# Splitting queries and keys before the transposition, with the orders of all engines rewritten

## The chip, the cores and the metric

The kernel runs on one core of a Trainium2 chip. The metric is the device time of one launch in microseconds (us). Five engines work side by side, each through its own list of instructions in order: TensorE (PE), VectorE (DVE), ScalarE (ACT), GpSimd (POOL) and SyncE (SP, which here only issues DMA). They wait for each other by semaphores.

## The reference, cut to what matters

```python
h = concat([tok(x), txt], axis=1)       # 64 images; 196 patches + 32 text rows = 228 tokens of 192
xn = norm_scale * layernorm(h) + norm_bias
q, k, v = split(xn @ W_attn + b_attn)   # 12 heads of 16
q, k = rope(q), rope(k)                 # o0 = x0*cos - x1*sin ; o1 = x0*sin + x1*cos
att = softmax(concat([sink, causal(q @ k.T / 4)]))[..., 1:]
h = h + (att @ v @ W_proj + b_proj) * rezero
xf = layernorm(h)                       # mixture of 8 experts, the best 2 of each token
out = h + sum over 2 experts of w * expert(xf)     # a token keeps its slot while an expert has room
```

`tok` sums each 16x16 patch of 12 channels and multiplies by a 12x192 matrix. Everything is float32. The products of queries and keys, which feed an exponential, are formed from two parts of each number: the number rounded to the short format `fp32r`, and the remainder. So a head has 64 rows on the contraction side: 16 numbers in the four pairings of high and low parts.

## The kernel before, in words

The kernel has two passes. Pass 1 goes through the 64 images ("batches"), from the patches to the attention, the gate and the scatter of each token's row into the expert's list in HBM. Pass 2 goes through the lists of the 8 experts. The change touches pass 1 alone.

Pass 1 is a pipeline written by hand. One **step** of it works on five batches at once, each one stage further: `p` (image folded on POOL, pooled on DVE), `a` (layernorm, the product that gives q and k, the rotation), `m` (q and k turned so that a head's numbers lie along partitions, then first scores and their maxima), `t` (scores once more, transposed, exponentials, attention, projection) and `z` (second layernorm, gate, choice of two experts, slots, scatter). `batches()` gives them; `steps()` runs 6 steps unrolled, then a loop of two steps at a time to 64, then 4 steps of emptying. In a step, the order of instructions on each engine is that of `step_tensor`, `step_scalar`, `step_vector` and `pass1_gpsimd`, written out by hand. T0 to T5 are the six turns of q and k (`turn_qk`; even numbers turn q, odd ones k), S0 to S8 the nine transposed scores (`score_t`), and `score` 0 to 8 the first scores. These 24 products use the PSUM banks 0 to 3 in a ring (`RING`, `bank_free`): each may start when the product four places before it has been read. Banks 4 and 5 hold the attention, 6 and 7 the rest.

What the change touches, by name:

- `make_qk(t)` (L847) multiplies the normalized tokens of half `t` by the weights of q and k; half 0 goes to bank 6, half 1 to bank 7. `rotate` (L533, L535) multiplies the result by cosine and sine into `rot_c` and `rot_s` on DVE. `add_rotation` (L723) adds the two on POOL, in two instructions a half, and writes each sum four times into `qk`: 768 elements a partition each.
- `turn_qk` (L892) transposes four blocks of `qk` in float32. `round_qk` (L775, ACT) copies the turned bank to `rounded` as `fp32r`. `split_qk` (L550, L556, DVE) reads `rounded` and the bank and writes high or low part into `q_t` (two instructions of 64 partitions) or `k_t` (one of 128).
- `norm1_stats`, `norm2_stats` (DVE), `inverse_std` (POOL, four small dependent instructions for each of the two norms) and `norm1_apply`, `norm2_apply` (ACT, L738, L746) make the two layernorms. `turn_xn` (L838), `copy_xn` (L759) bring the first one to `make_qk`.
- `gate_logits` (L1015, PE), `choose` (L620 to L635), `weigh` (L641 to L656) and `assign` (L663 to L679, all DVE) are the gate; `hot_sum` (L635) and `seen` (L677, L679) add two operands that both lie in SBUF. `scatter_waits` (L1272) issues four indirect DMAs from POOL's queue, behind `routed` and `row_whole`.
- `fold_image` (L686, POOL, three of 896 elements), `pool_image` (L502, DVE), `spread_patches` (L694, POOL), `sum_channels` (L829, PE), `copy_h` (L731, L732, ACT) are the patches.

## Time and profile before

| | us |
|---|---|
| median of 3 runs | 3273.91 |
| lowest, highest | 3270.16, 3279.08 |
| the profiled execution, whole | 3278.84 |
| its span (first to last instruction) | 3277.0 |
| pass 1, to the last scatter's landing | about 2036 |

The page of the profile gives the busy time of each engine, the chain that ended last and the costliest groups of instructions. For a pipeline like this one the useful views are those of a single step: the timeline of each engine, with the idle time ahead of an instruction and what ended it. An engine's busy time includes time in which an instruction had started and stood, so a long duration may itself be a wait.

### The profile page before, as it was taken

The page shows a single profiled execution, that of the slowest core. Times are in us where ns is not written, and L with a number is a line of the kernel's source. Part 1 is how long each engine was busy: PE and PEld are TensorE (multiplying, and loading weights), DVE is VectorE, ACT ScalarE, POOL GpSimd, SP SyncE. Part 2 cuts the span into 40 slices and gives each one's busy share as a digit, 9 for nine tenths or more (in the row PEclk, how much of TensorE's full clock was granted, in tenths as well). Part 3 has the DMA queues.
Part 4 walks back from the last instruction along what each step waited for, and adds up shares of the span by engine and source line. Part 5 has one row for each costly group of instructions (what it writes and reads, how often), then busy time and mean ns, then how long its engine had stood idle before and what let it go on. Part 6 is the DMA issues. An engine that isn't in the chain of part 4 may idle for free.

```text
span 3277.0 us, 62705 instructions
## 1 busy us (share of the span) xinstructions
PE 2888.8 (88%) x20432; PEld 2525.7 (77%) x20432; DVE 2329.4 (71%) x5748; ACT 1389.0 (42%) x3462; POOL 2082.0 (64%) x1814
## 2 busy tenths in 40 slices
PE   2888888888888888888888885999999999999997
PEld 1777777777777777777777774898988889898987
DVE  3888898898889889888988983445444545454453
ACT  0444444444444444444444443434343434443443
POOL 2677777777777777777777762455555555555555
PEclk9999999999999999999999996999999999999999
DMA  6545544433343343343333301333343343333333
GB/s 191 150 140 147 160 142 142 134 102 87 105 107 89 97 106 103 86 105 107 89 97 106 105 26 48 58 50 66 47 68 65 50 67 46 68 48 68 49 65 47
DMA packets 205961, 297.49 MB, mean 91 GB/s; under 512 B 88374, under 2 KB 167675, under 8 KB 205874
## 3 DMA queue, kind: packets, MB, share of 16 engines
q1 hardware_dynamic: 82994, 243.82, 26.9%
q0 software_dynamic: 122880, 52.55, 11.5%
q8 instruction: 50, 0.82, 0.1%
q14 instruction: 37, 0.30, 0.0%
HBM read 201.73 MB, written 93.90 MB: 90 GB/s over the span
## 4 chain that ended last, share of the span: by engine, by line
issue 29%; POOL 27%; PE 18%; DMA 13%; DVE 7%; ACT 4%; POOLq 1%; SPq 1%; DVEq 0%; ACTq 0%
DMA out<-arena,who 11%; POOL out L1441 8%; POOL qk L723 7%; POOL moe_rows L1272 6%; POOL spread L694 3%; DVE arena L1423 2%; PE bank L847 2%; PE bank L892 2%; PE bank L965 2%; ACT xn L738 2%; POOL rstd L707 1%; PE bank L1413 1%; PE bank L1015 1%; PE bank L838 1%; ACT prob L793 1%
## 5 line engine op out<-in xcount | busy, mean ns | idle before, releaser
L1441 POOL DMA_INDIRECT out<-arena,who x320 | 598.1, 1869 | 203.5 <-issue 199.3
L723 POOL TENSOR_TENSOR qk<-rot_c,rot_s 114x768 f32<-114x768 f32 x256 | 456.4, 1808 | 240.7 <-DVE rot_s L535 238.2
L1399 ACT ACTIVATE arena<-bank 128x456 f32<-128x456 f32 x320 | 175.5, 549 | 629.8 <-PE bank L1390 625.0
L1413 PE MATMUL bank<-prob,arena 128*114 128x192 f32 x2560 | 429.3, 326 | 0.0
L686 POOL TENSOR_TENSOR arena<-arena 112x896 f32<-112x896 f32 x192 | 396.5, 2092 | 44.6 <-DMA arena<-in_x 44.6
L1413 PEld LDWEIGHTS bank<-prob,arena 128*114 128x114 f32 x2560 | 412.2, 178 | 0.0
L1405 DVE TENSOR_TENSOR arena<-bank,arena 128x456 f32<-128x456 f32 x320 | 201.6, 630 | 263.9 <-ACT arena L1399 261.6
L1272 POOL DMA_INDIRECT moe_rows<-row,slot x256 | 293.0, 1144 | 103.1 <-issue 103.1
L571 DVE TENSOR_REDUCE top<-bank 114x2 f32<-114x456 f32 (+1 forms) x576 | 331.7, 623 | 1.8 <-PE bank L907 1.7
L1430 POOL TENSOR_TENSOR rms<-rms,minus_half 114x4 f32<-114x4 f32 x82 | 85.3, 1040 | 351.1 <-DVE rms L1328 351.1
L1386 PE MATMUL bank<-pieces 128*128 128x456 f32 x640 | 256.7, 401 | 44.4 <-DVE arena L1405 39.0
L550 DVE SCALAR_TENSOR_TENSOR pieces<-rounded,split,bank 64x456 fp32r<-64x456 f32 x384 | 261.6, 681 | 15.2 <-ACT rounded L775 10.1
L502 DVE TENSOR_REDUCE pooled<-arena 112x14 f32<-112x896 f32 x192 | 207.2, 1079 | 81.7 <-POOL arena L686 81.7
L1335 DVE COPY w_slot<-arena 114x4 f32 (+1 forms) x81 | 13.8, 171 | 331.8 <-DMA out<-arena,who 331.7
L790 ACT ACTIVATE prob<-bank 115x456 f32<-115x456 f32 x384 | 211.0, 550 | 88.4 <-PE bank L941 88.4
L775 ACT ACTIVATE rounded<-bank 128x456 fp32r<-128x456 f32 x384 | 210.6, 549 | 69.6 <-PE bank L892 68.7
L1388 PE MATMUL bank<-pieces 128*128 128x456 f32 x640 | 239.8, 375 | 0.0
L1390 PE MATMUL bank<-pieces 128*128 128x456 f32 x640 | 239.6, 374 | 0.0
L1387 PE MATMUL bank<-pieces 128*128 128x456 f32 x640 | 239.5, 374 | 0.0
L1389 PE MATMUL bank<-pieces 128*128 128x456 f32 x640 | 238.9, 373 | 0.0
L892 PE MATMUL bank<-ident,qk 114*128 114x114 f32 x1536 | 224.0, 269 | 5.8 <-POOL qk L723 5.8
L847 PE MATMUL bank<-w_qkv,xn_t 97*114 97x384 f32 x512 | 197.4, 509 | 21.7 <-DVE slot L674 21.1
(167 smaller groups left out, 7119.6 us busy)
## 6 DMA issues: line engine op xcount, KB each, us to landing
arena<-in_x SPq DMA_DIRECT2D x64, 2352.0 KB, 11.3
arena<-moe_rows SPq DMA_DIRECT2D x82, 363.4 KB
moe_rows<-filler SPq DMA_DIRECT2D x20, 1453.5 KB
out<-h SPq DMA_DIRECT2D x64, 171.0 KB
out<-arena,who POOLq DMA_INDIRECT x320, 5.1
arena<-in_w_t SPq DMA_DIRECT2D x9, 512.0 KB, 6.7
arena<-in_w_t SPq DMA_DIRECT2D x18, 256.0 KB, 7.2
moe_rows<-row,slot POOLq DMA_INDIRECT x256, 3.3
```

Of the source, the lines that this page charges most:

```text
L550: ins = nc.vector.scalar_tensor_tensor(out=dst, in0=hi[lo, :].bitcast(fp32).rearrange("p (a n) -> p a n", a=2), scalar=split[lo, 0:1], in1 ...
L571: nc.vector.tensor_reduce(dst, src, AX.X, ALU.max).then_inc(maxed[k], 1)
L686: nc.gpsimd.tensor_tensor(xin[at.par][:, g, 0:mid], xin[at.par][:, g, 0:mid], xin[at.par][:, g, mid:XF], ALU.add).then_inc(x_folded, 1)
L723: nc.gpsimd.tensor_tensor(dst, a, b, ALU.add).then_inc(qk_rotated[t], 1)
L847: ins = nc.tensor.matmul(bank[6 + t][0:TT, 0:2 * D], xn_t[:, c, TT * t:TT * (t + 1)], w_qkv[:, c, 0:2 * D], start=(c == 0), stop=(c == 1))
L892: ins = nc.tensor.transpose(dst[:, TT * (2 * a + t):TT * (2 * a + t + 1)], src, ident[0:TT, 0:TT])
L1272: nc.gpsimd.indirect_dma_start(out=moe_rows[0:SLOTS, :], out_offset=bass.IndirectOffsetOnAxis(ap=slot[at.par][:, 2 * t + k:2 * t + k + 1], ...
L1386: nc.tensor.matmul(dst, hi[:, 0, col], za_hi[:, :], start=True, stop=False)
L1388: nc.tensor.matmul(dst, lo[:, 0, col], za_hi[:, :], start=False, stop=False)
L1390: ins = nc.tensor.matmul(dst, lo[:, 1, col], zb[:, :], start=False, stop=True)
L1413: ins = nc.tensor.matmul(bank[6 + s // 2][0:TT, D * (s % 2):D * (s % 2 + 1)], hid[:, j, TT * s:TT * (s + 1)], w_dn[e_par][:, j, :], start= ...
L1441: nc.gpsimd.indirect_dma_start(out=out[:, :], out_offset=bass.IndirectOffsetOnAxis(ap=who[par][:, s:s + 1], axis=0), in_=ys[par][:, s, :], ...
```

## The change

- After `add_rotation`, which now adds in place and once (`rot_c`), ACT rounds the sum into the high places of `qk` (`high_parts`), and POOL subtracts to get the low ones (`low_parts`). `qk` is `fp32r`, and the turn is an `fp32r` product with a unit matrix. What comes out needs only a copy: `place_q` on ACT (two instructions) for q, `place_k` on DVE (one) for k. `round_qk` and `split_qk` are gone.
- Both halves of `make_qk` use bank 6, so the second waits for `rotate(0)`, and `make_v` for `rotate(1)`. Bank 7 is left to the shift and the gate.
- The orders in a step are new on PE, ACT, DVE and POOL. The scatter of a batch is issued one step later, at the head of POOL's step, and pass 1 on POOL has one step more.

The orders in a step, where it matters here. PE: T0, `turn_shift`, `sum_channels`, T1, S0, T2, S1, S2, T3, S3, S4, `attend` 0, T4, `turn_xn`, S5, `make_qk` 0, `turn_xf`, S6, `attend` 1, `make_qk` 1, `gate_logits`, T5, S7, S8, `score` 0, `rank`, `score` 1, `attend` 2, and the rest. ACT: q of T0, shift, `copy_h`, S0, q of T2, S1, S2, S3, `norm1_apply`, S4, `copy_xn`, `norm2_apply`, q of T4, S5, `copy_xf`, S6, `exp_gap`, `high_parts` 0, S7, S8, `keep_h`, `copy_y`, `high_parts` 1, `copy_yn`, `copy_v`. DVE: shift, both statistics and `place_k` 1 and 3, `rotate` 0, `choose`, `rotate` 1, `place_k` 5, maximum 0, `pool_image` 0, maximum 1, `weigh`, `pool_image` 1, maximum 2, `normalize`, `assign`, maxima 3 to 5, `pool_image` 2, maxima 6 to 8, `make_shift`, `residual`. The diff shows the start of each of these lists.

```diff
+        qk = sb("qk", [TT, 2, 2 * HEADS, 4, HD], fp32r)
         val = [sb(f"val{i}", [TT + 1, 2, HEADS, 32]) for i in range(2)]
-        rounded = [sb(f"rounded{i}", [128, 4 * TT], fp32r) for i in range(2)]
...
-            wait(dve, qk_rotated[t], 2 * at.b)
-            src = bank[6 + t][0:TT, 0:2 * D]
+            wait(dve, qk_low[t], at.b)
+            src = bank[6][0:TT, 0:2 * D]
...
-        def split_qk(dve, at, r):
-
-            dve.wait_ge(qk_rounded, 6 * at.b + r + 1)
...
+        def place_q(act, at, r):
+
+            act.wait_ge(qk_turned[r], at.b + 1)
+            if r == 0:
+                wait(act, scored_t[8], at.b - 1)
             k = TURNS[r]
-            if r == 0:
+            src = bank[bank_of("turn", r)]
+            for side in range(2):
+                lo = slice(64 * side, 64 * side + 64)
+                dst = q_t[at.par][lo, :, :].rearrange("p (a s) n -> p a s n", s=2)[:, 2 * k:2 * k + 2, side, :]
+                ins = nc.scalar.activation(dst, src[lo, 0:4 * TT].rearrange("p (a n) -> p a n", a=2), ACT.Copy)
+            ins.then_inc(qk_placed[r], 1)
...
+        def place_k(dve, at, r):
+
+            dve.wait_ge(qk_turned[r], at.b + 1)
+            if r == 1:
                 wait(dve, scored_t[8], at.b - 1)
...
-            else:
-                kk = k - 3
-                dst = k_t[at.par][:, 2 * kk:2 * kk + 2, :, 0:TT].rearrange("p a t n -> p (a t) n")
-                ins = nc.vector.scalar_tensor_tensor(
-                    out=dst, in0=hi[:, :].bitcast(fp32).rearrange("p (a n) -> p a n", a=4), scalar=split[:, 1:2],
-                    in1=src[:, 0:4 * TT].rearrange("p (a n) -> p a n", a=4), op0=ALU.mult, op1=ALU.add)
-            ins.then_inc(qk_split[r], 1)
+            kk = TURNS[r] - 3
+            dst = k_t[at.par][:, 2 * kk:2 * kk + 2, :, 0:TT].rearrange("p a t n -> p (a t) n")
+            src = bank[bank_of("turn", r)][:, 0:4 * TT].rearrange("p (a n) -> p a n", a=4)
+            nc.vector.tensor_copy(dst, src).then_inc(qk_placed[r], 1)
...
         def add_rotation(pool, at, t):
-            n = at.b + 1
-            pool.wait_ge(qk_read[t], n)
-            if t == 0:
-                wait(pool, qk_turned[5], at.b)
+
+            pool.wait_ge(qk_read[t], at.b + 1)
             for half in range(2):
-                dst = qk[:, t, :, :, 8 * half:8 * half + 8]
-                a = rot_c[:, t, :].rearrange("p (a s k) -> p a s k", s=2, k=8)[:, :, half, :].unsqueeze(2)
-                b = rot_s[:, t, :].rearrange("p (a s k) -> p a s k", s=2, k=8)[:, :, 1 - half, :].unsqueeze(2)
-                a, b = (v.to_broadcast([TT, 2 * HEADS, 4, 8]) for v in (a, b))
-                nc.gpsimd.tensor_tensor(dst, a, b, ALU.add).then_inc(qk_rotated[t], 1)
-
+                c, sn = (r[:, t, :].rearrange("p (a s k) -> p a s k", s=2, k=8)[:, :, i, :]
+                         for r, i in ((rot_c, half), (rot_s, 1 - half)))
+                ins = nc.gpsimd.tensor_tensor(c, c, sn, ALU.add)
+            ins.then_inc(qk_rotated[t], 1)
+
+        def low_parts(pool, at, t):
+
+            pool.wait_ge(qk_high[t], at.b + 1)
+            for hi, lo, of, first in piece_views(t):
+                ins = nc.gpsimd.tensor_tensor(lo, of, first.bitcast(fp32), ALU.subtract)
+            ins.then_inc(qk_low[t], 1)
+
+        def piece_views(t):
+
+            for side in range(2):
+                heads = slice(HEADS * side, HEADS * (side + 1))
+                of = rot_c[:, t, D * side:D * (side + 1)].rearrange("p (a k) -> p a k", k=HD)
+                of, first = (v.unsqueeze(2).to_broadcast([TT, HEADS, 2, HD]) for v in (of, qk[:, t, heads, 0, :]))
+                if side == 0:
+                    parts = qk[:, t, heads, :, :].rearrange("p a (c s) k -> p a s c k", s=2)
+                else:
+                    parts = qk[:, t, heads, :, :].rearrange("p a (s c) k -> p a s c k", s=2)
+                yield parts[:, :, 0, :, :], parts[:, :, 1, :, :], of, first
+
+
+        def high_parts(act, at, t):
+
+            act.wait_ge(qk_rotated[t], at.b + 1)
+            wait(act, qk_turned[5], at.b)
+            for hi, lo, of, first in piece_views(t):
+                ins = nc.scalar.activation(hi, of, ACT.Copy)
+            ins.then_inc(qk_high[t], 1)
...
-                wait(pe, routed, at.b - 2)
+                pe.wait_ge(qk_read[0], n)
             for c in range(2):
-                ins = nc.tensor.matmul(bank[6 + t][0:TT, 0:2 * D], xn_t[:, c, TT * t:TT * (t + 1)], w_qkv[:, c, 0:2 * D],
...
-            pe.wait_ge(qk_read[0], n)
+            pe.wait_ge(qk_read[1], n)
...
-                pe.wait_ge(qk_rotated[1], 2 * n)
-                pe.wait_ge(qk_rotated[0], 2 * n)
+                pe.wait_ge(qk_low[1], n)
+                pe.wait_ge(qk_low[0], n)
...
-                    ins = nc.tensor.transpose(dst[:, TT * (2 * a + t):TT * (2 * a + t + 1)], src, ident[0:TT, 0:TT])
+                    ins = nc.tensor.matmul(dst[:, TT * (2 * a + t):TT * (2 * a + t + 1)], src, ident_r[0:TT, 0:TT],
+                                           start=True, stop=True)
...
-            pe.wait_ge(qk_read[1], after(at))
+            wait(pe, routed, at.b - 1)
...
-            half1("S0 T2 S1 S2 T3")
+            half1("T1 S0 T2 S1 S2 T3 S3 S4")
+            if t:
+                attend(pe, t, 0)
+            half1("T4")
+            if a:
+                turn_xn(pe, a)
+            half1("S5")
+            if a:
+                make_qk(pe, a, 0)
...
-            half1("S0 T2 S1")
+            half1("S0 T2 S1 S2 S3")
+            if a:
+                norm1_apply(act, a)
+            half1("S4")
+            if a:
+                copy_xn(act, a)
...
         def step_vector(dve, p, a, m, t, z):
-            if m:
-                split_qk(dve, m, 0)
             if t:
                 split_shift(dve, t)
             if z:
                 norm2_stats(dve, z)
             if m:
-                split_qk(dve, m, 1)
+                place_k(dve, m, 1)
             if a:
...
                 rotate(dve, a, 0)
             if z:
-                assign(dve, z)
+                choose(dve, z)
+            if a:
+                rotate(dve, a, 1)
             if m:
-                split_qk(dve, m, 5)
...
         def pass1_gpsimd(pool):
             def one(half, par, known=None, fill=None):
                 p, a, _, t, z = batches(half, par, known)
+                done = Batch(half, par, 5) if known is None or 0 <= known - 5 < B else None
+                if done:
+                    scatter_waits(pool, done, fill)
+                if a:
+                    inverse_std(pool, a, norm1)
                 if z:
                     inverse_std(pool, z, norm2)
-                if a:
-                    inverse_std(pool, a, norm1)
                 if p:
-                    for g in range(NG):
-                        fold_image(pool, p, g)
+                    fold_image(pool, p, 0)
+                    fold_image(pool, p, 1)
                 if a:
                     add_rotation(pool, a, 0)
-                if z:
-                    scatter_waits(pool, z, fill)
+                if p:
+                    fold_image(pool, p, 2)
                 if a:
+                    low_parts(pool, a, 0)
                     add_rotation(pool, a, 1)
+                    low_parts(pool, a, 1)
                 if p:
                     spread_patches(pool, p)
...
-            for i in range(B, B + 4):
+            for i in range(B, B + 5):
...
```

How instructions lie in a row, at three places. POOL, one step inside the loop of pass 1, from the folds to the spreading (the scatter is `moe_rows`). Before:

```order
L686 TENSOR_TENSOR arena<-arena 112x896 [waits x_loaded0] x3
L723 TENSOR_TENSOR qk<-rot_c,rot_s 114x96x8 [waits qk_turned5,qk_read0]
L723 TENSOR_TENSOR qk<-rot_c,rot_s 114x96x8
L1262 ISA
L1268 REGISTER_ALU [waits filled0]
L1272 DMA moe_rows<-row,slot 36480x204 [waits row_whole,routed]
L1272 DMA moe_rows<-row,slot 36480x204 x3
L723 TENSOR_TENSOR qk<-rot_c,rot_s 114x96x8 [waits qk_read1]
L723 TENSOR_TENSOR qk<-rot_c,rot_s 114x96x8
L693 ISA
L694 TENSOR_TENSOR spread<-pooled,patch 112x196 [waits x_pooled]
```

After, the same stretch; the third fold stands between the addition and the subtraction of half 0:

```order
L686 TENSOR_TENSOR arena<-arena 112x896 [waits x_loaded0] x2
L719 TENSOR_TENSOR rot_c<-rot_c,rot_s 114x24x8 [waits qk_read0]
L719 TENSOR_TENSOR rot_c<-rot_c,rot_s 114x24x8
L686 TENSOR_TENSOR arena<-arena 112x896 [waits x_loaded0]
L726 TENSOR_TENSOR qk<-rot_c,qk 114x24x16 [waits qk_high0]
L726 TENSOR_TENSOR qk<-rot_c,qk 114x12x32
L719 TENSOR_TENSOR rot_c<-rot_c,rot_s 114x24x8 [waits qk_read1]
L719 TENSOR_TENSOR rot_c<-rot_c,rot_s 114x24x8
L726 TENSOR_TENSOR qk<-rot_c,qk 114x24x16 [waits qk_high1]
L726 TENSOR_TENSOR qk<-rot_c,qk 114x12x32
L693 ISA [waits h_summed]
L694 TENSOR_TENSOR spread<-pooled,patch 112x196 [waits x_pooled]
```

The scatter has left this stretch, and each half waits for ACT (`qk_high`). It stands now at the head of the step, POOL after:

```order
L1268 UNCONDITIONAL_BRANCH
L1282 ISA [waits filled1]
L1286 DMA moe_rows<-row,slot 36480x204 [waits row_whole,routed]
L1286 DMA moe_rows<-row,slot 36480x204 x3
L703 ISA
L705 TENSOR_TENSOR var<-mv,ln_eps 114x2 [waits ln1_done,ln1_step]
```

So the first layernorm's `inverse_std` stands right behind the scatter. DVE, the middle of a step in the loop, where the gate and the rotation meet (`best` is the gate's choice, `pieces` is where q and k are split). Before:

```order
L635 TENSOR_TENSOR hot_sum<-hot 114x16
L540 REGISTER_ALU
L550 SCALAR_TENSOR_TENSOR pieces<-rounded,split,bank 64x2x228 x2
L641 TENSOR_SCALAR gden<-gexp 114x2
L642 REGISTER_ALU
L643 RECIPROCAL gw<-gden 114x2
L644 REGISTER_ALU
L645 TENSOR_TENSOR gw<-gexp,gw 114x2
L648 TENSOR_TENSOR wpick<-hot,gw 114x32
L651 REGISTER_ALU
L652 TENSOR_TENSOR row<-wpick 114x2x8
L653 CAST row<-token 114x2
```

`rotate` of half 0 follows there, and right behind it `assign`. After:

```order
L533 TENSOR_TENSOR rot_c<-bank,cos 114x384
L535 TENSOR_TENSOR rot_s<-bank,sin 114x384
L620 MAX best<-bank 114x8 x2
L624 MAX_INDEX best_i<-best,bank 114x8 x2
L627 CAST bank<-best_i 114x4
L628 ISA
L629 TENSOR_TENSOR hot<-small,bank 114x32
L633 REGISTER_ALU
L635 TENSOR_TENSOR hot_sum<-hot 114x16
L533 TENSOR_TENSOR rot_c<-bank,cos 114x384
L535 TENSOR_TENSOR rot_s<-bank,sin 114x384
L559 CAST pieces<-bank 128x4x114
```

Both rotations now lie around the choice, and what was a split in two instructions is one copy from PSUM, for k alone. The gate's weights and the slots come later in the step, behind maxima.

## Rows read from the trace of the kernel before

**Rows 1.** Busy time by stretch, middle of pass 1: each engine's us and (instructions).

```profile
core 0: us, PE busy (x) PEld busy (x) DVE busy (x) ACT busy (x) POOL busy (x), PEclk, DMA share, GB/s
900.00:1100.00 200.00, 175.05 (x1434) 146.79 (x1434) 180.49 (x428) 90.02 (x201) 145.39 (x150) 1.00 0.39 101
```

**Rows 2.** Line L578, one per step: duration ns min/median/max, first and last start.

```profile
L578 DVE TENSOR_TENSOR shift<-top,sink_tok x64: 207/689/1682, 102.1 to 1990.6; 114x48 f32<-114x48 f32 x64
```

**Rows 3.** POOL timeline, one step: start, us, instruction, count, [idle before <-releaser].

```profile
911.64 1.47 POOL L694 TENSOR_TENSOR spread<-pooled,patch 112x196 f32<-112x196 f32 x3
916.13 0.20 POOL L705 TENSOR_TENSOR var<-mv,ln_eps 114x2 f32<-114x2 f32 x1 [3.02 <-DVE mv L519]
...
919.12 6.21 POOL L686 TENSOR_TENSOR arena<-arena 112x896 f32<-112x896 f32 x3
929.10 3.56 POOL L723 TENSOR_TENSOR qk<-rot_c,rot_s 114x768 f32<-114x768 f32 x2 [3.77 <-DVE rot_s L535]
932.87 1.20 POOL L1272 DMA_INDIRECT moe_rows<-row,slot  x1 [0.21 <-issue]
...
938.37 3.57 POOL L723 TENSOR_TENSOR qk<-rot_c,rot_s 114x768 f32<-114x768 f32 x2
```

**Rows 4.** DVE timeline, the same step.

```profile
922.59 0.25 DVE L620 MAX8 best<-bank 114x8 f32<-114x8 f32 x2 [0.26 <-PE bank L1015]
...
923.83 1.54 DVE L635 TENSOR_TENSOR hot_sum<-hot 114x16 bf16<-114x16 f32 x1
925.29 1.38 DVE L550 SCALAR_TENSOR_TENSOR pieces<-rounded,split,bank 64x456 fp32r<-64x456 f32 x2
...
928.00 0.56 DVE L533 TENSOR_TENSOR rot_c<-bank,cos 114x384 f32<-114x384 f32 x1
...
928.94 0.17 DVE L663 TENSOR_SCALAR over<-bank 114x16 f32<-114x16 f32 x1
...
929.88 1.04 DVE L677 TENSOR_TENSOR seen<-seen,hot_sum 114x8 bf16<-114x8 bf16 x1
930.95 1.73 DVE L679 TENSOR_TENSOR seen<-seen,hot_sum 114x8 bf16<-114x8 bf16 x1
932.60 0.68 DVE L556 SCALAR_TENSOR_TENSOR pieces<-rounded,split,bank 128x456 fp32r<-128x456 f32 x1
933.20 1.07 DVE L502 TENSOR_REDUCE pooled<-arena 112x14 f32<-112x896 f32 x1
...
936.20 0.22 DVE L593 RECIPROCAL rden<-bank 114x12 f32<-114x12 f32 x1
...
937.39 2.24 DVE L571 TENSOR_REDUCE top<-bank 114x4 f32<-114x456 f32 x4
```

**Rows 5.** ACT timeline, the same step.

```profile
919.54 0.98 ACT L738 ACTIVATE xn<-h,shifted,rstd 114x192 f32<-114x192 f32 x2
...
921.28 0.55 ACT L759 ACTIVATE xn_t<-bank 97x456 f32<-97x456 f32 x1
```

**Rows 6.** PE timeline, the same step.

```profile
920.57 0.63 PE L838 MATMUL bank<-ident,xn 114*97 114x114 f32 x4 [0.62 <-ACT xn L738]
...
921.56 0.87 PE L1015 MATMUL bank<-gate,xf_t 96*114 96x8 f32 x8
922.37 0.61 PE L965 MATMUL bank<-prob,val 115*32 115x228 f32 x8
...
923.11 0.61 PE L892 MATMUL bank<-ident,qk 114*128 114x114 f32 x4
...
924.33 1.50 PE L847 MATMUL bank<-w_qkv,xn_t 97*114 97x384 f32 x4
925.37 0.67 PE L938 MATMUL bank<-pieces 128*115 128x456 f32 x1
```

**Rows 7.** DVE timeline while pass 1 empties.

```profile
2001.46 0.17 DVE L635 TENSOR_TENSOR hot_sum<-hot 114x16 bf16<-114x16 f32 x1
...
2005.37 0.16 DVE L679 TENSOR_TENSOR seen<-seen,hot_sum 114x8 bf16<-114x8 bf16 x1
```

**Rows 8.** POOL timeline behind it.

```profile
2006.37 1.18 POOL L1272 DMA_INDIRECT moe_rows<-row,slot  x1 [11.64 <-issue]
```

More of the change, by code:

```diff
@@ L766, in copy_v @@
                                  bank[6][0:TT, 0:2 * D].rearrange("p (a k) -> p a k", k=HD), ACT.Copy).then_inc(v_ready, 1)
-        def round_qk(act, at, r):
-            n = at.b + 1
-            act.wait_ge(qk_turned[r], n)
-            if r >= 2:
-                act.wait_ge(qk_split[r - 2], n)
-            else:
-                wait(act, qk_split[r + 4], at.b)
-            nc.scalar.activation(rounded[r % 2][:, :], bank[bank_of("turn", r)][:, 0:4 * TT], ACT.Copy).then_inc(qk_rounded, 1)
         def round_shift(act, at):
@@ L1079, in step_tensor @@
             if m:
-                score(pe, m, t, 3)
-            if m:
-                for k in range(4, 6):
+                for k in range(3, 6):
                     score(pe, m, t, k)
@@ L1086, in step_tensor @@
             if m:
-                score(pe, m, t, 6)
-                score(pe, m, t, 7)
-                score(pe, m, t, 8)
+                for k in range(6, 9):
+                    score(pe, m, t, k)
             if t:
@@ L1145, in step_vector @@
             if m:
[L1146 to L1156 removed]
+                place_k(dve, m, 3)
             if a:
@@ L1159, in step_vector @@
             if z:
-                assign(dve, z)
+                choose(dve, z)
+            if a:
+                rotate(dve, a, 1)
             if m:
-                split_qk(dve, m, 5)
+                place_k(dve, m, 5)
+                max_scores(dve, m, 0)
+            if p:
+                pool_image(dve, p, 0)
+            if m:
+                max_scores(dve, m, 1)
+            if z:
+                weigh(dve, z)
             if p:
@@ L1173, in step_vector @@
                 normalize(dve, t, 1)
+            if z:
+                assign(dve, z)
             if m:
-                for k in range(2, 6):
+                for k in range(3, 6):
                     max_scores(dve, m, k)
```

83 lines of the change are left out of this document (24 added, 59 removed).

## The prediction

> **What bounds the kernel now.** I first read how long a step of pass 1 is, because the change lies in that loop alone. L578 runs once a step, its 64 executions start from 102.1 to 1990.6, so a step is 1888.5 / 63 = 29.98 us [rows 2]. Then the busy time: in 200 us in the middle DVE is busy 180.5, PE 175.1, POOL 145.4, ACT 90.0 [rows 1], that is 27.1, 26.2, 21.8 and 13.5 us a step. No engine is full. So I read POOL's timeline, whose waits say which loop closes: in a step it stands 3.02 us for the layernorm's statistics and 3.77 us for `rot_s` [rows 3]. Everything else on it is back to back: spreading 1.47, two norms 2.99 (916.13 to 919.12), folds 6.21, addition 3.56, four scatters 5.5 (932.87 to 938.37), addition 3.57.
>
> Why `rot_s` is late is in DVE's timeline [rows 4]. Its product was issued on PE at 924.33 and took 1.50 [rows 6], so it was there at 925.83; DVE came to it at 928.00, behind the choice, a split and the weights. Three of DVE's instructions are long for their size. `hot_sum`, 16 elements, takes 1.54 us, and `seen`, 8 elements, 1.04 and 1.73. When POOL is still, `hot_sum` takes 0.17 and `seen` 0.16 [rows 7]. The three end with a POOL instruction: 923.83 + 1.54 = 925.37 is the end of the folds (919.12 + 6.21 = 925.33), 929.88 + 1.04 = 930.92 is half of the additions begun at 929.10, 930.95 + 1.73 = 932.68 their end at 932.66 [rows 3, 4]. So DVE instructions with both operands in SBUF wait out the running POOL instruction, 1.37 + 0.88 + 1.57 = 3.8 us a step. The Trainium skill says so too (SBUF — State Buffer, section "Who interferes with whom": a DVE instruction with two SBUF inputs contends with a GpSimd instruction that reads SBUF, and the later one is blocked); by that rule the trace agrees. The loop that closes a step is thus: DVE's queue up to `rotate` 0, POOL from there to the spreading, channel sum, statistics, norm, q and k, DVE again.
>
> **The change, part by part.** *DVE.* Three split pairs of 1.38 and three splits of 0.68 go: -6.2 us. Three copies of 456 elements out of PSUM come. The trace has no such copy; the bounds are the maximum, a single read of 456 elements from PSUM at 2.24 / 4 = 0.56, and the split itself at 0.68 [rows 4]. I take 0.57, since the copy too has one source: +1.7.
>
> *ACT.* Six roundings become six half-height copies, the same count of the same 456 elements: 0 net. `high_parts` adds four instructions of 384 elements; bounds are 0.49 (192 elements, SBUF) and 0.55 (456, PSUM) [rows 5]: +2.0 us, on an engine that is busy 13.5 of 30. Their place matters more: POOL waits for them twice a step.
>
> *POOL.* Four additions of 768 elements (7.1 us) become four of 192 and four subtractions of 384. Spreading with 196 elements costs 0.49, 768 cost 1.78, so 384 lie near 0.95: 2.2 + 3.8 = 6.0 [rows 3]. I keep 0.8 to 1.2 for a subtraction. POOL's own work falls from 23.3 to 22.2.
>
> *PE.* The same six turns in another format: before, four blocks start 0.37 apart as a whole (923.11 to the next start) and their end is hidden. I take no change; were each turn 0.2 longer, PE would have 1.2 us more in a step where it stands about 3.8.
>
> *The scatter* moves from between the two additions to the head of the step. It fills the 3.02 us wait for statistics, and what it delays is now the norm behind it. Its lead is new: when POOL stands, the first scatter starts 1.0 behind the last `seen` started (2005.37 to 2006.37), so some 1.1 behind its release, the slots just ahead [rows 7, 8]; before, the additions covered that (idle 0.21 [rows 3]). The third spreading (0.49) covers less than half of it.
>
> *The last bank.* `make_qk` 1 waits for `rotate` 0, and the gate's logits stand behind `make_qk` 1 on PE. So `choose`, and with it DVE's whole second half, now waits for the rotation chain.
>
> **The new step, walked through.** I lay the new orders out with these durations; 0 is the start of the first norm's `inverse_std`.
> - Norm on POOL: 2.99 / 2 = 1.5. ACT takes `norm1_apply` behind S3's exponential, at 1.9 (0.3 for that queue): 0.98, ends 2.9. Turn on PE to the start of `copy_xn`: 0.71 (920.57 to 921.28) [rows 5, 6]. It ends at 4.2, `make_qk` 0 takes 1.50, `rotate` 0 from 5.8 to 6.8.
> - ACT behind `copy_xn`: `norm2_apply` 0.98, q of T4 1.0, S5's exponential 0.55, done 6.5. `attend` 1 0.74 (922.37 to 923.11), `make_qk` 1 1.04 (924.33 to 925.37), logits 0.87 [rows 6]. `choose` starts at 9.3.
> - DVE, all its own: up to `hot_sum` 1.24 and 0.2 for it, `rotate` 1 0.94 (928.00 to 928.94), copy 0.57, six maxima 0.54 each 3.25, three poolings 1.0 each, weights 1.3 (from 925.29 + 1.38 to 928.00), `normalize` 1.2 (936.20 to 937.39), `assign` 0.94 (928.94 to 929.88) and 0.4 for `seen`: 13.0 [rows 4]. `pool_image` 2 ends at 22.4.
> - Spreading and lead 1.1, scatters 5.5: `inverse_std` starts again at 29.0.
>
> POOL meanwhile: norms to 3.0, two folds to 7.1, addition 8.3, fold 10.4, subtraction 10.9 (after ACT) to 12.8, addition 13.9, and it stands for `high_parts` 1, which ACT reaches behind `copy_y`: subtraction 15.4 to 17.4. The next T0 needs it at about 24, so both ACT waits are hidden, by 6 us. In this layout `hot_sum` (10.5) just clears the fold (10.4), the weights (14.3 to 15.6) fall into POOL's gap, and `seen` (19.1) into the next: of the 3.8 us almost nothing is left.
>
> The second loop, DVE's own, from `pool_image` 2 through three maxima, `make_shift`, channel sum, `copy_h` and statistics (1.6 + 0.2 + 4.3) gives 28.4. So 29.0 by the scatter, 28.4 without its lead. I take 29.0, a gain of 0.98. DVE loses 8 us of load and gets only one back, because it now waits some 4 us for `rotate` 0 and 2.5 for the gate.
>
> **Sum.** About 60 of the 63 periods are full ones: 60 x 0.98 = -59. While pass 1 empties, `assign` stands behind `normalize` and the last but one scatter lies ahead of the last norm: +2. Pass 2 is the same instructions: 0. Against the profiled execution, 3278.8 - 57 = 3221.8; that execution is 4.9 above the median, so some 3218.
>
> **The rivals.** *The waits for POOL come back* (slower). The weights have three two-operand instructions and `seen` two. They clear POOL's subtractions by 0.2 to 1 us in my layout. If `low_parts` lies under them, each waits out up to one subtraction (0.95), and `seen` could again pay 0.88 + 1.57 [rows 3, 4]. From 1.0 us of this a step the gain is gone; at 2 us a step is 31.0, 60 x 1.0 = +60: 3334. For it: the margins are less than I can lay out by hand. Against it: POOL now stands about 7 us a step, and a delay of DVE doesn't delay POOL's subtractions. Chance 0.2.
>
> *The chain is shorter than laid out* (much faster). The lead of the scatter may overlap the spreading wholly, and ACT's queue may not hold the norm: 28.4 - 0.6 and less elsewhere, about 27.6: 60 x 2.4 = -144, 3130. PE's 26.2 busy us stand against more. Chance 0.17.
>
> *It does nothing*: the step stays within 0.15 us of 29.98, because the new dependence of the gate on the rotation costs what DVE gained; 3274. Chance 0.1.
>
> The Trainium skill has a price for the copies (VectorE: DVE Perf Modes, the errata section: 120 cycles and one per element at 0.96 GHz out of PSUM). By it a copy of 456 elements would take 0.60 us, an estimate from that page, and the step would be 0.03 longer; no row here shows it.
>
> **How the numbers follow.** The forecast has 0.53, the rivals 0.2, 0.17 and 0.1. Of the forecast's own spread, 28.4 to 29.7 us a step, 3182 to 3262, all is faster. The range of 8 in 10 takes in half of each outer rival: 3150 to 3300. A measurement of this kernel can tell about 0.3%, 10 us, from no change. Faster 0.53 + 0.17 = 0.7, same 0.1, slower 0.2.
>
> **What would show each step.** The spacing of the `shift` instruction near 29.0; `hot_sum` and `seen` near 0.17 instead of 1.54, 1.04 and 1.73; DVE idle about 4 us ahead of L533 and 2 to 3 ahead of the choice; POOL's first norm idle nearly 0, directly behind the scatter; `place_k` near 0.57 and the subtraction near 0.95. The prediction is wrong if the two-operand instructions stay long, if POOL waits for ACT ahead of T0, or if PE, not DVE, stands ahead of `make_shift`.

## The result, and the profile after

| | before | after |
|---|---|---|
| median of 4 runs, us | 3273.55 | 3349.51 |
| lowest, highest | 3270.16, 3279.08 | 3333.55, 3369.78 |
| the profiled execution, whole | 3278.84 | 3338.47 |

The ratio is 1.0233, with a 95% interval of 1.0200 to 1.0265. The change makes the kernel 2.3% slower. The forecast was 3218, with a range of 3150 to 3300.

The loss lies in the steps of pass 1. The line that runs once a step, in the listing by line (duration in ns min/median/max, first and last start in us), after the change:

```profile
L578 DVE TENSOR_TENSOR shift<-top,sink_tok x64: 207/209/251, 107.2 to 2057.9; 114x48 f32<-114x48 f32 x64
```

(2057.9 - 107.2) / 63 = 30.96 us a step, against 29.98 [rows 2]. That is 63 x 0.98 = 62 us, and the two profiled executions differ by 59.6 (the medians by 76; the profiled execution of after is one of its two shorter ones). The step was to become 0.98 shorter and became 0.98 longer.

The same 200 us as in [rows 1], busy time by stretch (us and instructions of PE, its weight loads, DVE, ACT, POOL, then PE's granted clock, the DMA share, GB/s), after:

```profile
900.00:1100.00 200.00, 179.73 (x1365) 157.12 (x1363) 117.62 (x369) 95.01 (x217) 129.58 (x162) 0.91 0.33 91
```

DVE's load fell from 180.5 to 117.6 us, POOL's from 145.4 to 129.6, in the direction forecast. PE is busier, with fewer instructions (1365 for 1434), and the clock column reads 0.91, where [rows 1] had 1.00. The page's line of the clock in 40 slices (a digit is tenths of full speed, so 9 also stands for 1.00), first before, then after, has an 8 in several slices of pass 1, the first 24 or so:

```profile
PEclk9999999999999999999999996999999999999999
```

```profile
PEclk8899999998989999998999899799999999999999
```

Three single steps of after, cut at L578, by the same view:

```profile
1294.34:1323.94 29.60, 26.38 (x222) 22.75 (x221) 18.64 (x59) 15.35 (x35) 20.43 (x27) 1.00 0.36 101
1012.11:1043.23 31.12, 27.90 (x222) 24.41 (x221) 18.67 (x59) 15.43 (x35) 21.34 (x27) 0.94 0.35 95
943.68:977.92 34.24, 31.08 (x221) 27.29 (x220) 18.71 (x59) 15.45 (x35) 21.39 (x27) 0.85 0.32 86
```

With the same instructions a step takes 29.6 us at full clock, 31.1 at 0.94 and 34.2 at 0.85, and the whole difference is PE's busy time (26.38, 27.90, 31.08), while DVE's stays at 18.6 to 18.7. So there are two results to explain: a step at full clock is 29.6 rather than 29.0, and most steps aren't at full clock.

Where the clock falls is seen in PE's windows of 1.5 us (us, PE busy and instructions, clock, DMA share, GB/s):

```profile
936.00:937.50 1.50, 0.68 (x7) 1.00 0.00 0
937.50:939.00 1.50, 0.73 (x7) 1.00 0.00 0
939.00:940.50 1.50, 0.71 (x6) 1.00 0.00 0
940.50:942.00 1.50, 1.50 (x7) 0.51 0.00 0
942.00:943.50 1.50, 1.50 (x6) 0.50 0.55 72
...
949.50:951.00 1.50, 1.50 (x8) 0.58 1.04 309
951.00:952.50 1.50, 1.50 (x15) 1.00 1.03 289
```

From 936.0 to 940.5 PE is busy for 2.12 of 4.50 us. Behind that the clock is 0.50, that is 1.2 of 2.4 GHz, for about 10 us in which PE works without a pause. PE's timeline (start, us, instruction, count, idle ahead of it and what ended it) names the waits and what is slow behind them:

```profile
938.27 0.63 PE L1004 MATMUL bank<-ident,yn 114*97 114x114 f32 x4 [1.59 <-DVE yn L598]
...
940.02 0.47 PE L929 MATMUL bank<-pieces 128*114 128x228 f32 x2 [0.79 <-DVE top L571]
...
941.28 2.77 PE L1012 MATMUL bank<-w_out,yn_t 97*114 97x192 f32 x8
943.84 2.77 PE L871 MATMUL bank<-w_qkv,xn_t 97*114 97x192 f32 x8
...
1291.63 1.47 PE L1012 MATMUL bank<-w_out,yn_t 97*114 97x192 f32 x8
```

`turn_yn` waits 1.59 us for `normalize`, and `score` 7 0.79 for a maximum to free its bank. Neither is long. `project` and `make_v`, which come next, take 2.77 each and start 2.56 apart; in the undisturbed step (the last row) `project` takes 1.47 and `make_v` starts 1.30 behind it. The fall doesn't follow these waits every time: from 700 to 1300 us it does in 15 of 19 steps. Before, the waits of a step stood further apart:

```profile
930.10 1.52 PE L847 MATMUL bank<-w_qkv,xn_t 97*114 97x384 f32 x4 [0.34 <-DVE slot L674]
...
933.42 0.44 PE L904 MATMUL bank<-mask_q,ident_r 114*114 114x456 f32 x1 [1.06 <-DVE pieces L556]
...
937.52 0.63 PE L988 MATMUL bank<-ident,yn 114*97 114x114 f32 x4 [0.61 <-DVE yn L598]
```

The 4.5 us of before around its longest wait, by the view of the windows:

```profile
928.90:933.40 4.50, 3.12 (x28) 1.00 0.14 39
```

PE stands about as long in a step of after at full clock (29.60 - 26.38 = 3.2 us) as before (30.0 - 26.2 = 3.8). Before has six waits over 0.25 us in each step between 700 and 1300, the longest 1.1; after has three, and its two longest end 1.75 us apart. So the waits have come together, right ahead of the products on which the next step hangs: 2.12 us of work in 4.50, where before has 3.12 around its longest wait.

### The profile page after: what moved, and what is told of

It reads as the page before. It is cut to its first block, busy times and chain, and to the rows that moved or that the text cites. A ratio compares the mean times of both kernels' runs of the same rounds, so it can differ in the third digit from the quotient of the medians.

```text
span 3336.7 us, 62374 instructions
## 1 busy us (share of the span) xinstructions
PE 2977.3 (89%) x20432; PEld 2661.1 (80%) x20432; DVE 1805.7 (54%) x5364; ACT 1483.0 (44%) x3718; POOL 2020.1 (61%) x2070
## 4 chain that ended last, share of the span: by engine, by line
PE 44%; DVE 19%; issue 15%; DMA 12%; POOL 9%; SPq 1%; DVEq 1%; POOLq 0%; ACT 0%; ACTq 0%
DMA out<-arena,who 10%; POOL out L1455 8%; PE bank L862 6%; DVE top L571 5%; PE bank L844 5%; PE bank L907 4%; PE bank L1012 4%; PE bank L871 3%; DVE arena L1437 2%; PE bank L954 2%; PE bank L981 2%; PE bank L956 2%; PE bank L929 2%; PE bank L1427 2%; PE bank L1031 1%
## 5 line engine op out<-in xcount | busy, mean ns | idle before, releaser
L726 POOL TENSOR_TENSOR qk<-rot_c,qk 114x384 fp32r<-114x384 f32 x256 | 252.6, 1007 | 193.2 <-ACT qk L747 193.2
L907 PE MATMUL bank<-ident_r,qk 114*128 114x114 f32 x1536 | 252.5, 288 | 2.3 <-POOL qk L726 2.3
L533 DVE TENSOR_TENSOR rot_c<-bank,cos 114x384 f32<-114x384 f32 x128 | 70.9, 554 | 295.0 <-PE bank L862 295.0
L907 PEld LDWEIGHTS bank<-ident_r,qk 114*128 114x128 f32 x1536 | 216.1, 197 | 15.5 <-issue 11.6
L694 POOL TENSOR_TENSOR spread<-pooled,patch 112x196 f32<-112x196 f32 x192 | 96.8, 517 | 211.6 <-DVE pooled L502 211.6
L929 PE MATMUL bank<-pieces 128*114 128x228 f32 x768 | 174.0, 322 | 49.2 <-DVE top L571 49.2
```

What stands on the lines that cost most here:

```text
L726: ins = nc.gpsimd.tensor_tensor(lo, of, first.bitcast(fp32), ALU.subtract)
L907: ins = nc.tensor.matmul(dst[:, TT * (2 * a + t):TT * (2 * a + t + 1)], src, ident_r[0:TT, 0:TT], start=True, stop=True)
L929: nc.tensor.matmul(dst[0:TT, T * a:T * (a + 1)], q_t[at.par][:, hh, TT:T], k_t[at.par][:, kk, :, 0:TT], start=(a == 0), stop=False, skip_g ...
```

## The experiments

The theory: the waits bunched ahead of `turn_yn` and `score` 7 bring PE's clock down, and that, not any new wait, makes the change slower. The rivals: the clock is a bystander and the new order is slower by itself; or the low clock comes from the new `fp32r` turns or from load, and would be there however the waits lie. "Idle products" are 128x128 matrix products on PE into an unused part of bank 6, which nobody reads. They take 0.12 us each. Steps below are worked out from L578 as above; the clock is that of the 600 us from 700 to 1300. Each ratio is to runs of before made beside that kernel, whose medians lie between 3273.1 and 3277.9.

| | median, us | ratio to before (95%) | step, us | clock |
|---|---|---|---|---|
| before | 3273 | 1 | 29.98 | 1.00 |
| after | 3349.5 | 1.0233 (1.0200 to 1.0265) | 30.96 | 0.92 |
| e1b: after, 16 + 8 idle products in the waits | 3253.5 | 0.9932 (0.9908 to 0.9956) | 29.58 | 1.00 |
| f1: after, the first 16 alone | 3247.4 | 0.9918 (0.9901 to 0.9935) | 29.52 | 1.00 |
| f2: after, the other 8 alone | 3314.5 | 1.0137 (1.0112 to 1.0161) | 30.60 | 0.95 |
| f3: after, 24 behind the waits | 3724.8 | 1.1361 (1.1325 to 1.1397) | 37.67 | 0.82 |
| e2b: before, 16 + 8 at the same places | 3351.1 | 1.0240 (1.0219 to 1.0262) | 31.15 | 1.00 |
| e5: before, `normalize` late | 3450.7 | 1.0544 (1.0526 to 1.0561) | 32.80 | 0.96 |
| g1: e5, 20 idle products in its wait | 3372.3 | 1.0290 (1.0273 to 1.0307) | 31.51 | 1.00 |
| e3: after, two poolings early | 3255.7 | 0.9957 (0.9940 to 0.9973) | 29.40 | 0.97 |
| e4: e3, 4 + 12 idle products | 3204.6 | 0.9786 (0.9766 to 0.9806) | 28.80 | 1.00 |
| g2: after, all poolings early | 3258.5 | 0.9949 (0.9931 to 0.9966) | 29.74 | 0.98 |
| e8: g2, `assign` behind maximum 5 | 3101.1 | 0.9472 (0.9453 to 0.9491) | 27.23 | 1.00 |
| f4: e1b, scatter in its own step | 3520.0 | 1.0762 (1.0741 to 1.0782) | 33.77 | 0.95 |

**e1b: fill the waits.**

```diff
+        def idle_work(pe, a, read, n):
+            if not a:
+                return
+            pe.wait_ge(qk_read[read], a.b + 1)
+            for _ in range(n):
+                nc.tensor.matmul(bank[6][:, 384:512], ident_r[:, :], ident_r[:, :], start=True, stop=True)
...
+                idle_work(pe, a, 1, 16)
                 turn_yn(pe, t)
...
-                for k in range(6, 9):
-                    score(pe, m, t, k)
+                score(pe, m, t, 6)
+                idle_work(pe, a, 1, 8)
+                score(pe, m, t, 7)
+                score(pe, m, t, 8)
```

> The changed kernel with 24 idle products a step (128x128 in fp32r, into bank 6, which is free at that point; nothing reads them), 16 of them where TensorE waits ahead of turn_yn and 8 where it waits ahead of score 7. Theory A (the quiet of TensorE there makes its clock fall to half over the projection, v, the first turn and the channel sum): granted clock 1.00 through pass 1, the projection 1.3 us instead of 2.6, every step near the 29.6 us of the undisturbed ones, total 3278.8 - 63 x 0.4 = about 3255. Theory B (the new order's chain alone costs the time; the clock falls for another reason and hides behind waits): clock still near 0.94, step 31 us or more because TensorE has more to do, total 3345 to 3380.

3253.5 us: more work, and 96 us less than after. L578 and two rows of PE's timeline:

```profile
L578 DVE TENSOR_TENSOR shift<-top,sink_tok x64: 207/208/249, 107.7 to 1971.0; 114x48 f32<-114x48 f32 x64
```

```profile
1022.68 1.90 PE L1054 MATMUL bank<-ident_r 128*128 128x128 f32 x16
...
1025.23 1.01 PE L1054 MATMUL bank<-ident_r 128*128 128x128 f32 x8
```

The products fill both waits, the steps are 29.6 but for one (35.6, around 621 us, with the clock down) and those at the two ends of the pass, the clock from 700 to 1300 is 1.00, and the same `fp32r` turns run. So the turns don't bring the clock down, and load doesn't either. At full clock the change is worth 20 us (0.7% by the ratio); the clock takes 96.

**e2b: the same filling in the kernel before.** The edit is that of e1b, on the kernel before; there `idle_work` waits for `qk_read[0]`, since bank 6 holds half 0 alone.

> Control: the same 24 idle products at the same two places of the kernel before, whose clock is 1.00 in pass 1 anyway. Theory A: they fit the waits there only in part (0.6 us ahead of turn_yn), so 0 to +1.5 us a step, 3273 to 3370, and no gain. A gain over 10 us would say that idle products help for another reason than the clock.

3351.1, 78 us slower than before. There the clock was 1.00 already, so nothing was to be won, and the 24 products had no wait of their size to lie in: 1.17 of their 2.9 us a step lie on the path. Idle products are no good in themselves.

**f1 and f2: one of the two places each.** The edits are the first and the second call of e1b alone.

> The changed kernel with idle products in the first wait of TensorE alone: 16 ahead of turn_yn, none ahead of score 7. Theory A says that what counts is how quiet TensorE is in the few us ahead of the projection, the longer wait (1.6 us) more than the shorter (0.8): clock 0.97 or more in pass 1, most steps 29.6 us, total 3250 to 3290. If both waits are needed: clock below 0.96, total 3300 or more.

> The changed kernel with idle products in the second wait alone: 8 ahead of score 7. Theory A: the longer wait ahead of turn_yn stays, so the clock still falls in a part of the steps, clock 0.95 to 0.98, total 3275 to 3335, between the fill of the first wait alone and the changed kernel.

With the 16 products ahead of `turn_yn` alone the clock is 1.00 and the time (3247.4, where 3250 to 3290 was expected) slightly under e1b's; by this run the change is worth 26 us at full clock, and the clock takes 102. The 8 ahead of `score` 7 give back 35 of the 96 us. It is the wait for `normalize` that decides; the other one adds to it.

**f3: the same 24 products behind the waits**, between `project` and `make_v`.

```diff
             if t:
                 project(pe, t)
+            idle_work(pe, a, 1, 24)
             if a:
                 make_v(pe, a)
```

> The changed kernel with all 24 idle products between the projection and v, where TensorE has no wait. Theory A: they come after the quiet, so the clock falls as before, and they lie on the path: 2.9 us a step at full clock and up to 5.8 at half, 3530 to 3650, granted clock in pass 1 not above that of the changed kernel by much. Rival (any more work for TensorE in a step holds its clock): clock 1.00, step 29.6 + 2.9, total 3435.

3724.8, above what was expected (3530 to 3650). Its profiled execution, from which the step and the clock are, took 3766.4, 1% over the median. The busy time from 700 to 1300:

```profile
700.00:1300.00 600.00, 552.25 (x3791) 495.27 (x3791) 285.43 (x900) 242.16 (x548) 325.11 (x406) 0.82 0.30 82
```

The same number of products that gave 96 us in the waits costs 375 behind them. A step is 6.7 us longer than after's by the profiles, 6.0 by the medians. Most of it is the products themselves: in a step with the fall they take 5.47 us together, where e1b's take 2.91. The rest is other work at the low clock, whose mean is 0.82 for 0.92. In these runs work that came once the clock was down did not bring it back sooner; work in the waits kept it up.

**e5 and g1: make the wait in the kernel before, then fill it.** In e5 `normalize` stands behind maximum 5 in the old order. g1 adds 20 idle products ahead of `turn_yn`.

```diff
             if m:
                 for k in range(2, 6):
                     max_scores(dve, m, k)
+            if t:
+                normalize(dve, t, 0)
+                normalize(dve, t, 1)
```

> The kernel before with one edit on DVE: normalize stands behind maximum 5 instead of behind maximum 1, so turn_yn waits some 2.2 us longer and TensorE is quiet there. Theory A: the clock falls in pass 1 of this kernel too (below 0.98), the projection takes 2.6 us instead of 1.3 in many steps, step 31.5 us or more, total 3370 to 3450. Theory B: clock stays 1.00, only the later end of the attention counts, 0 to 1.5 us a step, 3275 to 3370.

> The kernel of e5_before_norm_late (normalize behind maximum 5, clock 0.97 in the middle of pass 1, 3450) with 20 idle products ahead of turn_yn, where TensorE waits 2.8 us. Theory A (quiet brings the clock down): clock 1.00, steps near its shortest, 31.7 us, instead of 32.8 in the mean, total about 3380; what stays over 3273 is the late attention itself. Rival (the later attention alone makes the time): clock unchanged at 0.97, 3450 or more.

PE's windows in e5, with the wait, and the row behind it in its timeline (columns as in those of after):

```profile
1042.50:1044.00 1.50, 0.89 (x6) 1.00 0.26 62
1044.00:1045.50 1.50, 0.00 (x0) 1.00 0.23 63
1045.50:1047.00 1.50, 0.65 (x6) 1.00 0.23 63
1047.00:1048.50 1.50, 1.50 (x10) 0.55 0.20 24
```

```profile
1046.35 0.63 PE L988 MATMUL bank<-ident,yn 114*97 114x114 f32 x4 [2.77 <-DVE yn L598]
```

3450.7, at the very top of what was expected. The old turns, the old order everywhere else, and the mean clock falls to 0.96; filled (g1) it is 1.00 again. Here too the fall doesn't follow every time: one step earlier the same wait, 2.78 us to 1014.72, is followed by 1.00 up to 1019.5. Why a wait is followed by it in one step and not in the next stays open. Of e5's loss of 177 us the clock is about 80 (3450.7 to 3372.3 is 78), and the rest is the late attention itself. This rules out that the low clock belongs to the changed kernel alone.

**e3 and e4: the same work in another order.** e3 moves `pool_image` 0 and 1 on DVE into the wait for the gate's logits, between `rotate` 0 and `choose`, where DVE stood 3.08 us. So `normalize` comes earlier. e4 adds 4 and 12 idle products.

```diff
                 rotate(dve, a, 0)
+            if p:
+                pool_image(dve, p, 0)
+                pool_image(dve, p, 1)
             if z:
                 choose(dve, z)
...
-            if p:
-                pool_image(dve, p, 0)
...
-            if p:
-                pool_image(dve, p, 1)
```

> The changed kernel with pool_image 0 and 1 moved on DVE from behind maxima 0 and 1 to between rotate 0 and choose, where DVE waits 3.1 us for the gate. Nothing else. The loop of a step is TensorE from score 8 to the gate's logits, then DVE from the choice to maximum 4; this takes 2.0 us out of its DVE half. If that loop sets the step and the clock holds: 27.6 to 28 us, total about 3145 to 3175. If the clock still falls as in the changed kernel: 1.4 us a step more, about 3235 to 3260. If DVE's load as a whole were the bound, and not this loop: no difference, 3340.

> The kernel of e3_pool_early (pool_image 0 and 1 ahead of the choice), whose steps were 28.85 us where the clock held and 30.3 to 33.5 where it fell, mean 29.40, with idle products in its two waits of TensorE: 4 ahead of turn_yn, 12 ahead of score 7. Theory A: clock 1.00 and 28.9 us in every step, total 3278.8 - 63 x 1.1 = about 3210. Theory B: no gain on 3256, or a loss of up to 1 us a step.

PE's two waits in e3:

```profile
1039.88 0.63 PE L1004 MATMUL bank<-ident,yn 114*97 114x114 f32 x4 [0.22 <-DVE yn L598]
...
1042.20 0.47 PE L929 MATMUL bank<-pieces 128*114 128x228 f32 x2 [1.36 <-DVE top L571]
```

The wait for `normalize` has gone from 1.59 to 0.22, that of `score` 7 has grown from 0.79 to 1.36, and the clock is 0.97 instead of 0.92. Both the order and the clock pay: e3 takes 94 us less than after without a single instruction more or less, and with the rest of the clock's loss filled (e4) another 51. At clock 1.00 on both sides the order alone is worth 49 (e1b's 3253.5 to e4's 3204.6).

At full clock a step of e3 is 28.8, where 27.6 to 28 was expected: 2.0 us of pooling left the stretch, and only 0.8 was won. DVE now stands 0.43 for a first score, and the POOL waits are back in part. `seen` falls on POOL's spreading and takes 0.45 and 0.44 instead of 0.15 and 0.16, in g2 and e4 as well:

```profile
1040.68 0.45 DVE L677 TENSOR_TENSOR seen<-seen,hot_sum 114x8 bf16<-114x8 bf16 x1
1041.16 0.44 DVE L679 TENSOR_TENSOR seen<-seen,hot_sum 114x8 bf16<-114x8 bf16 x1
```

**g2 and e8: take the waits away.** g2 moves all three poolings ahead of `choose`, for which the third fold goes ahead of `add_rotation` 0 on POOL. The wait ahead of `score` 7 is for maximum 3, which stands behind `assign`; e8 also puts `assign` behind maxima 3 to 5. The diff is e8's without the three poolings; of what it shows, g2 has the third fold, and `pool_image` 2 gone from its old place.

```diff
-            if z:
-                assign(dve, z)
             if m:
                 for k in range(3, 6):
                     max_scores(dve, m, k)
-            if p:
-                pool_image(dve, p, 2)
+            if z:
+                assign(dve, z)
...
                     fold_image(pool, p, 1)
+                    fold_image(pool, p, 2)
                 if a:
                     add_rotation(pool, a, 0)
-                if p:
-                    fold_image(pool, p, 2)
-                if a:
```

> The kernel of e8_all_early (27.2 us a step, 3101) with assign back at its place ahead of maximum 3: only the three poolings and the third fold are early. If the stretch from the choice to maximum 4 closes the loop, assign's 1.4 us come back in part: 27.8 to 28.6 us a step, and the wait ahead of score 7 with them; if the clock then falls in some steps, up to 29: total 3150 to 3210. If the place of assign does not matter: 3101.

> The changed kernel with all three pool_image ahead of the choice on DVE, the third fold ahead of add_rotation 0 on POOL, and assign behind maximum 5. No idle products. It takes 3.0 us of pooling out of the stretch from the choice to make_shift and 1.4 more out of the one to maximum 4. If the two loops through DVE and TensorE set the step and the clock holds: 27.6 to 27.9 us, total 3130 to 3150. TensorE then has 26 us of work in 27.7, so theory A lets its clock hold better than in e3_pool_early (mean granted clock over 0.964). If the clock falls as often as there: 28.2 to 28.6, 3165 to 3195. Theory B (the wait for the rotation and the gate is what costs, and pooling in it delays the choice): no gain on 3256.

Both missed what was expected: g2 took 3258.5 (3150 to 3210), e8 3101.1 (3130 to 3150 at full clock). g2's row ahead of `score` 7, and then the waits of PE over 0.3 us or at `turn_yn` in a step of e8, with e8's L578:

```profile
1023.15 0.47 PE L929 MATMUL bank<-pieces 128*114 128x228 f32 x2 [1.29 <-DVE top L571]
```

```profile
1026.51 0.43 PE L920 MATMUL bank<-mask_q,ident_r 114*114 114x456 f32 x1 [0.68 <-DVE pieces L559]
...
1031.06 0.63 PE L1004 MATMUL bank<-ident,yn 114*97 114x114 f32 x4 [0.23 <-DVE yn L598]
```

```profile
L578 DVE TENSOR_TENSOR shift<-top,sink_tok x64: 207/208/517, 104.2 to 1819.6; 114x48 f32<-114x48 f32 x64
```

g2 alone gives no more than e3. The wait of 1.29 us is still there, and the clock is still 0.98. `assign`'s place is worth 157 us: in e8 the longest wait of PE between 700 and 1300 is 0.7 us, the clock there is 1.00 without any idle product, and the step is 27.23. `seen` is back at 0.15 and 0.16 there, so the place also takes it out from under the spreading. e8 is 5.3% faster than before and 7.4% faster than after. How much of the 157 us is the clock was not split by a run; g2's undisturbed steps are 28.8 to 29.0 us long and its mean 29.74, which puts some 0.8 of the 2.5 us a step on the clock. Which loop closes e8's step was not tested.

**f4: the scatter back in its own step**, between the last subtraction and the spreading, on e1b.

```diff
-                done = Batch(half, par, 5) if known is None or 0 <= known - 5 < B else None
-                if done:
-                    scatter_waits(pool, done, fill)
...
                     low_parts(pool, a, 1)
+                if z:
+                    scatter_waits(pool, z, fill)
...
-            for i in range(B, B + 5):
+            for i in range(B, B + 4):
```

> The scatter's move undone, on the kernel of e1b_fill (24 idle products, clock held, 29.58 us a step): the scatter of z stands in its own step again, behind the subtraction of half 1 and ahead of the spreading, since its slots are made by assign only then. The slots come about 9.9 us behind the choice, the scatter runs from 11.0 to 16.5, the spreading to 18, and the channel sum, which starts 15.0 behind the choice in e1b_fill, starts at 18: +3 us a step, 3255 + 63 x 3 = about 3440, and more if TensorE's wait there lets its clock fall. If the scatter's place does not matter in the new order: 3255.

3520.0, more than expected. POOL and PE, by timeline:

```profile
1013.70 1.20 POOL L1295 DMA_INDIRECT moe_rows<-row,slot  x1 [2.52 <-issue]
```

```profile
1020.73 2.59 PE L844 MATMUL bank<-chan,spread 112*114 112x192 f32 x9 [2.78 <-POOL spread L694]
```

POOL stands 2.52 us, 1.5 of it until the slots are written at 1012.67 and 1.0 more ahead of the first scatter; the spreading comes behind four scatters, and the channel sum waits 2.78 for it. The idle products don't cover that place, so the clock falls too (0.95). At this place in the new order the scatter costs 266 us, the lower clock included; the move to the next step is needed there.

## Why the prediction was wrong

**The step that failed is the one on PE.** The text took "no change" for PE's turns and then treated PE's busy time as fixed. The sum had no term for PE's clock, and no rival did. It was 1.00 in the stretch of [rows 1], and I took that as a given of the kernel, not as a result of how its waits lay. The forecast had DVE stand some 4 us for `rotate` 0 and 2.5 for the gate, and then work through a long queue with `normalize` near its end. I priced this for DVE alone, and didn't ask what PE does while DVE catches up. The answer was 2.4 us of standing in 4.5. After minus e1b says what it cost: 96 us of 3349.5. Less the 20 us that the change is worth at full clock, that is the measured +76. Of the 131 us between the forecast and the measured time the clock is 96, and the other 36 are the second thing that was mis-sized, the step at full clock.

The Trainium skill (TensorE: Matmul & The Clock Gate, section "HAM oscillation — how this bites in real kernels") describes a loop in which PE waits for data in each pass and starts each pass at the low clock. The trace agrees in kind: the clock falls behind the same waits in 15 of 19 steps. It differs in form: there the cause is one long wait for a transfer, here several short ones, the longest 1.59 us.

**The step at full clock: 29.58, not 29.0.** The chain of waits of after, one undisturbed step (start, us, what):

```profile
1290.67 0.47 PE bank L929 x2
...
1291.79 1.30 PE bank L1012 x8
...
1295.07 2.18 PE bank L844 x12
...
1304.03 1.41 PE bank L862 x4
...
1307.24 1.48 PE bank L862 x4
1308.71 0.73 PE bank L1031 x8
1309.59 0.26 DVE best L620 x2
```

```profile
1320.27 0.47 PE bank L929 x2
```

From `score` 7 at 1290.67 to the end of the gate's logits at 1309.44 PE works 18.8 us on end; then DVE goes from `choose` at 1309.59 through the weights, the attention's division and the slots to the maximum that frees the bank of `score` 7 at 1320.27. 18.8 + 10.8 = 29.6. I had laid out POOL's chain with care and PE's queue not at all: `turn_xn` stands on PE behind five turns, S0 to S4 and `attend` 0, which I passed over. By my loop POOL's scatter would close the step. It nearly does. POOL in the same step:

```profile
1298.19 1.12 POOL L1286 DMA_INDIRECT moe_rows<-row,slot  x1 [0.30 <-issue]
1299.34 0.20 POOL L705 TENSOR_TENSOR var<-mv,ln_eps 114x2 f32<-114x2 f32 x1
```

The norm stands right behind the last scatter with no idle time, as forecast; `xn` is there at 1302.44 (ACT, 1301.46 + 0.98), and PE reaches `turn_xn` at 1302.83. So the forecast loop is 0.4 shorter than the one that closes, about 29.2. That order of the two is read from this trace alone; no run tells them apart, since they share DVE's second half, and e3, whose undisturbed steps are 28.8, shortens both. `make_qk` was mis-sized as well: I took 1.50 and 1.04, from its first row and from the start of the next product; the chain has 1.41 and 1.48. Two slips of arithmetic cost nothing: 3221.8 less 4.9 is 3217, not 3218, and ACT is done at 6.7, not 6.5, which leaves `choose` at 9.3 to 9.4.

**What was right.** DVE's timeline after, the answers to [rows 4] and [rows 7]:

```profile
925.22 0.56 DVE L533 TENSOR_TENSOR rot_c<-bank,cos 114x384 f32<-114x384 f32 x1 [4.40 <-PE bank L862]
...
929.33 0.25 DVE L620 MAX8 best<-bank 114x8 f32<-114x8 f32 x2 [3.08 <-PE bank L1031]
...
930.57 0.18 DVE L635 TENSOR_TENSOR hot_sum<-hot 114x16 bf16<-114x16 f32 x1
...
931.59 0.62 DVE L559 CAST pieces<-bank 128x456 fp32r<-128x456 f32 x1
...
939.07 0.15 DVE L677 TENSOR_TENSOR seen<-seen,hot_sum 114x8 bf16<-114x8 bf16 x1
939.26 0.16 DVE L679 TENSOR_TENSOR seen<-seen,hot_sum 114x8 bf16<-114x8 bf16 x1
```

The instructions with two operands in SBUF no longer wait out POOL's: 0.18, 0.15 and 0.16 instead of 1.54, 1.04 and 1.73. The waits for `rotate` 0 and the gate are 4.40 and 3.08 (forecast about 4 and 2 to 3). The copy has 0.62 for a forecast of 0.57. POOL's parts, the answers to [rows 3]:

```profile
931.00 1.98 POOL L726 TENSOR_TENSOR qk<-rot_c,qk 114x384 fp32r<-114x384 f32 x2 [1.50 <-ACT qk L747]
932.93 1.15 POOL L719 TENSOR_TENSOR rot_c<-rot_c,rot_s 114x192 f32<-114x192 f32 x2
```

A subtraction takes 0.99 (forecast 0.95), an addition 0.58 (0.55). The terms of load held. They bought only 20 us at full clock. As I read the chain above, that is because a step closes over PE's queue and DVE's second half, behind the gate, where three poolings, the maxima and the slots still stood; e3 and e8, which only move work out of that stretch, agree with it.

**The rivals.** "The waits for POOL come back", the slower case, didn't happen in the change: `hot_sum` and `seen` have medians of 0.17, 0.15 and 0.16 us in after and in e1b. A slower kernel was given 0.2 for this reason, and came for another. The danger was real, though: in e3, e4 and g2 `seen` pays 0.5 us a step. "The chain is shorter than laid out" failed too, though e8 shows that the new parts allow 27.2 a step in a better order. The closing remark named "PE, not DVE, ahead of `make_shift`" as a sign that it would be wrong. `make_shift` still follows DVE's maxima with no idle time; what changed is behind it. Before, PE waited for its result in 62 of 64 steps, after in 2, because PE is still at its first turn when the result is there. That is the nearest the remark came to the cause, and no time stood behind it.

## What to carry to other kernels

When an order is rebuilt, write down for PE not only how long it stands in a step but where, and what comes right behind: here waits that gathered ahead of the critical products cost their own length and then the clock. Filling the waits with idle products for one run, and putting the same products elsewhere for another, splits a slowdown into order and clock. Idle time made on one engine (here DVE ahead of the gate) is the place for that engine's independent work; moving it there, with `assign` behind the maxima that PE waits for, turned a loss of 2.3% into a gain of 5.3%.

## What the runs showed of the hardware

- PE's clock fell from 2.4 to 1.2 GHz (1.00 to 0.50) though no wait was longer than 1.6 us; what stood ahead of the fall was 2.12 us of work in 4.50. Behind the same waits it fell in 15 of 19 steps.
- Once down it stayed there for about 10 us in the step shown, with PE busy throughout, and for less in others; 24 more products in that stretch (f3) made the mean clock lower, 0.82 for 0.92.
- Matrix products took about twice the time in such a stretch (`project` 1.47 to 2.77), while DVE and ACT kept theirs (18.64 and 15.35 us in the step at 1.00, 18.71 and 15.45 in the one at 0.85).
- DVE's small additions with both operands in SBUF took 0.15 to 0.18 us when POOL stood and up to 1.73 when they started under a POOL instruction, with whose end they ended. The order alone turned this off (after, e8) and on again (e3, g2: 0.45 and 0.44).
